# Input codes of a quantised feed-forward layer: two VectorE passes and a DMA transpose in place of a ScalarE pass, TensorE transposes and a PSUM copy

## What is computed

```python
def bit_linear(x, w, b):
    gamma_x = jnp.clip(jnp.max(jnp.abs(x), axis=-1, keepdims=True), 1e-05, None)
    scale_x = 127.0 / gamma_x
    x_dq = jnp.clip(jnp.round(x * scale_x), -128.0, 127.0) / scale_x
    gamma_w = jnp.clip(jnp.mean(jnp.abs(w)), 1e-05, None)
    w_dq = jnp.clip(jnp.round(w / gamma_w), -1.0, 1.0) * gamma_w
    return jnp.einsum('bsd,hd->bsh', x_dq, w_dq) + b
gate = jax.nn.silu(bit_linear(x, gate_w, gate_b))
val = bit_linear(x, val_w, val_b)
return bit_linear(gate * val, out_w, out_b)
...
x = x + jnp.tanh(g_xattn[0]) * cross_attention(layernorm(x), ctx, mask)
x = x + jnp.tanh(g_ffn[0]) * feed_forward(layernorm(x))
```

## Time and profile before

| | |
|---|---|
| median of the runs | 779.17 us (777.58 to 779.35) |
| the profiled execution | 779.99 us, of which the span is 778.2 us |
| TensorE (PE) busy | 712.3 us, 92% of the span |
| VectorE (DVE) busy | 623.1 us, 80% |
| ScalarE (ACT) busy | 534.4 us, 69% |
| GpSimd (POOL) busy | 316.6 us, 41% |
| mean granted clock of TensorE | 0.969 of full speed; full in all of the rows from 1 on |

### The profile page before, as it was taken

The page is one execution under the profiler, slowest core; times in us unless marked ns, Lnnn a source line. Parts: engine busy times, 40 slices in busy tenths (PEclk is TensorE's granted clock), DMA queues, the critical chain, the costliest instruction groups (busy, mean ns, idle before and its releaser), DMA issues.

```text
span 778.2 us, 13495 instructions
## 1 busy us (share of the span) xinstructions
PE 712.3 (92%) x4204; PEld 343.1 (44%) x4253; DVE 623.1 (80%) x1290; ACT 534.4 (69%) x701; POOL 316.6 (41%) x482
## 2 busy tenths in 40 slices
PE   4989756978989999999999999999999999999997
PEld 4434334333534454445444444444444444454443
DVE  6868797687878987798779877987798778778885
ACT  4576878877657865787668856795588657856554
POOL 4310315223553456344653454444544453354340
PEclk9989885989999999999999999999999999999999
DMA  9864426121553344534453354326433542243312
GB/s 323 257 222 123 107 102 205 35 42 41 114 113 79 82 110 94 115 81 103 99 115 81 66 123 101 81 68 126 104 75 83 118 92 65 55 91 80 88 42 67
DMA packets 177385, 81.05 MB, mean 104 GB/s; under 512 B 156595, under 2 KB 156851, under 8 KB 176710
## 3 DMA queue, kind: packets, MB, share of 16 engines
q1 hardware_dynamic: 177350, 80.62, 42.4%
HBM read 38.75 MB, written 10.51 MB: 63 GB/s over the span
## 4 chain that ended last, share of the span: by engine, by line
PE 43%; DVE 26%; issue 11%; ACT 7%; DMA 6%; POOL 3%; another core or an unknown queue 2%; SPq 1%; DVEq 0%; POOLq 0%; ACTq 0%
PE psum L1741 15%; PE psum L1707 12%; PE psum L1732 6%; DVE psum L1227 2%; DMA arena<-x_both 2%; ACT arena L921 2%; PE psum L1936 2%; PE psum L1711 2%; DVE stats L1266 2%; PE psum L1772 2%; DVE xmax L1312 2%; DVE delta L1285 1%; DVE stats L1300 1%; DVE delta L1294 1%
## 5 line engine op out<-in xcount | busy, mean ns | idle before, releaser
L1707 PE MATMUL psum<-ternary,xqT 128*128 128x512 f16 x1024 | 261.4, 382 | 3.3 <-DVE xqT L1257 1.1
L1707 PEld LDWEIGHTS psum<-ternary,xqT 128*128 128x128 f16 x1024 | 98.6, 99 | 119.8 <-issue 5.3
L665 POOL TENSOR_TENSOR rstd<-var_e,minus_half 128x1 f32<-128x1 f32 x64 | 39.8, 621 | 216.9 <-DVE var_e L1278 113.7
L1732 PE MATMUL psum<-ternary,arena 128*128 128x512 f16 x496 | 121.6, 379 | 2.1 <-DMA arena<-arena 2.1
L855 ACT ACTIVATE arena<-psum,dequant 128x512 f32<-128x512 f32 x128 | 86.3, 679 | 48.0 <-PE psum L1711 46.5
L1741 PE MATMUL psum<-wo_hi,arena 128*128 128x512 f16 x256 | 82.6, 384 | 1.0 <-issue 1.0
L1741 PE MATMUL psum<-arena,wq_hi 128*128 128x512 f16 x256 | 77.4, 385 | 3.1 <-DMA arena<-x_both 2.5
L1240 DVE TENSOR_REDUCE hmax<-arena 128x1 f32<-128x1024 f32 x64 | 77.6, 1213 | 0.8
L863 ACT ACTIVATE arena<-arena,round_c,hscale 128x1024 f32<-128x1024 f32 x62 | 73.5, 1235 | 1.9 <-DVE hscale L1252 1.9
L895 ACT ACTIVATE arena<-arena,round_c 128x1024 f16<-128x1024 f32 x62 | 70.8, 1143 | 0.3
L1732 PEld LDWEIGHTS psum<-ternary,arena 128*128 128x128 f16 x496 | 46.4, 98 | 55.0 <-issue 4.4
(11 more groups left out here) (214 smaller groups left out, 1308.5 us busy)
## 6 DMA issues: line engine op xcount, KB each, us to landing
arena<-in_x SPq DMA_DIRECT2D x64, 256.0 KB, 2.8
out<-arena SPq DMA_DIRECT2D x31, 256.0 KB, 2.3
arena<-in_L_ffn_gate_w SPq DMA_DIRECT2D x4, 1024.0 KB, 13.8
arena<-in_L_ffn_out_w SPq DMA_DIRECT2D x3, 1024.0 KB, 4.8
ternary<-in_L_ffn_val_w SPq DMA_DIRECT2D x2, 1024.0 KB, 11.4
kcur<-k_scratch SPq DMA_DIRECT2D x56, 32.0 KB, 2.2
arena<-arena SPq DMA_TRANSPOSE x90, 3.1
ternary<-in_ctx SPq DMA_DIRECT2D x1, 1024.0 KB, 5.4
```

Source lines behind the costliest of these rows:

```text
L1707: ins = M.matmul(ps[:], xqT[:, t % 2, k, :], w[:, k, cols], start=(k == 0), stop=(k == KC - 1 and not biased))
L1732: ins = M.matmul(psO[:], hidT[t % 2][:, k, :], wo2[:, k, :], start=(k == 0), stop=(k == FC - 1))
```

## The change

The codes are made by VectorE in two passes in the new `input_codes`, right behind `input_scale`: the first does what `round_input` did, the second takes the constant off and writes f16 to the new tile `xq16`. SyncE then transposes `xq16` into `xqT` by a DMA (`x_T`). TensorE's four transposes, VectorE's `xq_T` and ScalarE's `round_input` are gone. The product of the inverse scales stays where it was. `gate_val` waits for the codes alone at its start and for the inverse scales ahead of the first bias product.

```diff
+        xq16 = sb("xq16", [P, D], F16)
...
+            def x_T(row, t):
+                last, u = ahead(row, t, -2)
+                wait_alone(sp, s_met_sp, v_done, last, NCH * (u + 1))
+                wait_alone(sp, s_met_sp, xc16_ready, row, t + 1)
+                sp.dma_start_transpose(xqT[:, t % 2, :, :], xq16[:, :]).then_inc(xqT_loaded.sem, 16)
...
+                    x_T(0, 0)
                     sp.wait_ge(s_wtr, 6)
...
+                    update = att if t == NT - 1 else ffn
+                    if update and not (att and t == 2) and not (pre and t == 3):
+                        x_T(*ahead(b, t, 1))
                     if att and t == 2:
                         for u in range(NT):
+                            if u == C_T_AHEAD and update:
+                                x_T(*ahead(b, t, 1))
                             c_T(a, u)
                     if pre and t == 3:
                         h_T(c, 2)
+                        x_T(*ahead(b, t, 1))
...
             def update_inverse(row, t):
-                wait_alone(pool, s_met_pool, xq_tr, last, u + 1)
+                wait_alone(pool, s_met_pool, iv_tr, last, u + 1)
...
-                def round_input(row, t):
-                    wait(act, xq_tr, last, u + 1)
-                    wait(act, xs_ready, row, t + 1)
-                    A.activation(xq32, x1c, ACT.Identity, scale=xscale[:, t:t + 1],
-                                 bias=round_c[:, 0:1]).then_inc(xq_ready.sem, 1)
...
                 def inverse_rows(row, t):
-                    wait(act, xqT_ready, row, t + 1)
+                    wait(act, iv_tr, row, t + 1)
...
-                def xq_T(row, t):
-                    wait(dve, xq_tr, row, t + 1)
-                    V.tensor_scalar(xqT[:, t % 2, :, :].rearrange("p k n -> p (k n)"), half(psT)[:, 0:D], -HALF, None,
-                                    ALU.add).then_inc(xqT_ready.sem, 1)
...
+                def input_codes(row, t):
+                    last, u = ahead(row, t, -1)
+                    wait(dve, xc16_ready, last, u + 1)
+                    wait(dve, xs_ready, row, t + 1)
+                    V.tensor_scalar(xq32, x1c, xscale[:, t:t + 1], ROUND, ALU.mult, ALU.add).then_inc(xq_ready.sem, 1)
+                    wait(dve, xqT_loaded, last, 16 * (u + 1))
+                    wait(dve, xq_ready, row, t + 1)
+                    V.tensor_scalar(xq16[:, :], xq32, -ROUND, None, ALU.add).then_inc(xc16_ready.sem, 1)
...
                     if i == 0:
-                        wait(pe, xqT_ready, b, t + 1)
-                        wait(pe, iT_ready, b, t + 1)
+                        wait(pe, xqT_loaded, b, 16 * (t + 1))
...
-                        if m > 2:
-                            wait(pe, used, b, m - 2)
+                        wait(pe, used, *(b, m - 2) if m > 2 else (b - 1, NT * NCH + m - 2))
...
                         if biased:
+                            if i == 0:
+                                wait(pe, iT_ready, b, t + 1)
...
-                def xq_transpose(row, t):
-                    wait(pe, xq_ready, row, t + 1)
-                    codes = low(xq32)
-                    for k in range(KC):
-                        M.transpose(half(psT)[:, k * P:(k + 1) * P], codes[:, k * P:(k + 1) * P], eye16[:])
+                def inverse_transpose(row, t):
+                    last, u = ahead(row, t, -1)
+                    wait(pe, iT_ready, last, u + 1)
                     wait(pe, iv_part, row, PARTS * (t + 1))
                     M.matmul(psT[:, 2 * P:3 * P], inv_cols[:, t % 2, :], eye_b16[:],
-                             start=True, stop=True).then_inc(xq_tr.sem, 1)
+                             start=True, stop=True).then_inc(iv_tr.sem, 1)
...
+C_T_AHEAD = 2
```

More of the change, by code:

```diff
@@ L347, in build @@
         res_ready = per_row("resid_ready", NT)
-        xq_tr = per_row("xq_transposed", NT)
-        xqT_ready = per_row("xqT_ready", NT)
+        xc16_ready = per_row("x_codes_ready", NT)
+        iv_tr = per_row("inverse_transposed", NT)
+        xqT_loaded = per_row("xqT_loaded", 16 * NT)
         g_done = per_row("gate_product", NT * NCH)
@@ L864, in quant @@
                                      scale=hscale[:, t:t + 1], bias=round_c[:, 0:1]).then_inc(hq_ready.sem, 1)
-                def round_input(row, t):
-                    last, u = ahead(row, t, -1)
-                    wait(act, xq_tr, last, u + 1)
-                    wait(act, xs_ready, row, t + 1)
-                    A.activation(xq32, x1c, ACT.Identity, scale=xscale[:, t:t + 1],
-                                 bias=round_c[:, 0:1]).then_inc(xq_ready.sem, 1)
                 def inverse_rows(row, t):
-                    wait(act, xqT_ready, row, t + 1)
+                    wait(act, iv_tr, row, t + 1)
                     A.copy(inv_rows[:, t % 2, :], psT[:, 2 * P:3 * P]).then_inc(iT_ready.sem, 1)
@@ L962, in first_row @@
                     sum_abs(1, 3)
-                    round_input(0, 0)
                     round_w(0, 2)
@@ L993, in body @@
                     for n in range(NCH):
-                        if n == NCH - 1 and t == 0 and update:
-                            round_input(*ahead(b, t, 1))
                         if ffn:
@@ L1001, in body @@
                             h_high(c, 2)
-                        if n == NCH - 1 and t > 1 and update:
-                            round_input(*ahead(b, t, 1))
                         if att and t == 0:
@@ L1018, in body @@
                         exps(range(2))
-                        if update:
-                            round_input(*ahead(b, t, 1))
                         exps(range(2, NPAIR - 2))
                         exps(range(NPAIR - 2, NPAIR))
-                    if update and t == 1 and not att:
-                        round_input(*ahead(b, t, 1))
                     if pre and t != 2:
@@ L1384, in first_row @@
                     input_scale(0, 0)
+                    input_codes(0, 0)
                     weight_sum(1)
@@ L1394, in first_row @@
                     weight_clip(0, 2)
-                    xq_T(0, 0)
                     weight_round(0, 3)
@@ L1452, in body @@
                                 input_scale(*nxt)
+                                input_codes(*nxt)
                             if ffn and not (out_w_now and t == 1):
@@ L1456, in body @@
                             input_scale(*nxt)
+                            input_codes(*nxt)
                         if n == 3:
-                            if update and not att:
-                                xq_T(*nxt)
                             if ffn:
                                 hidden_max(t, 1)
-                            if update and att and t >= 2:
-                                xq_T(*nxt)
                         if att and t == 0 and n:
@@ L1470, in body @@
                             bound(i)
-                    if update and att and t < 2:
-                        xq_T(*nxt)
                     if out_w_now and t == 0:
@@ L1840, in first_row @@
                     weight_total(1)
-                    xq_transpose(0, 0)
+                    inverse_transpose(0, 0)
                     for g in range(SETUP_BANKS, W_GROUPS):
@@ L1894, in body @@
                     if update:
-                        xq_transpose(*nxt)
+                        inverse_transpose(*nxt)
                     if out_w_now and t == 0:
```

## The result

The changed kernel takes 792.67 us in the median of 4 runs (792.41 to 795.79), the kernel before 779.26 in the same comparison. The ratio is 1.018, with a 95% interval of 1.0146 to 1.0211. The direction was forecast (slower), the size was not: +13 us instead of +3.4, outside the range. The profiled execution took 792.77 us and its span is 791.0, 12.8 longer than before.

What follows compares the result with a forecast made beforehand. A row was taken as mostly TensorE-bound, with tiles 2 and 3 bound by VectorE, then GpSimd. Rows +1.4, setup +1.05, last row +0.94: +3.4 on 779.99, 783.4; less 0.8 for the profiled execution, 782.6 us; range 775.5 to 788.0.

Steps and rivals of the forecast that it cites:

- The step that failed: Tiles 0 and 1: VectorE's net +0.93 us a tile mostly covered, tile 1 by 2.04 us idle; gain 0.70 us a row.
- Rival D: Tiles 0 and 1: VectorE late, tile 0's extra not absorbed, gain falls to 0.2 us; 786.1 us, chance 0.10.
- Rival E: GpSimd's six: each pass blocks GpSimd for its full 0.48 us, 0.96 a tile; 790.2 us, chance 0.05.
- The gain: Tiles 0 and 1: project starts earlier without transposes and round_input; 0.70 us a row taken, bounds 0.2 and 0.92.
- GpSimd's six: Tiles 2 and 3: the passes delay GpSimd's six small instructions by 0.45 us each tile, counted once a row; bounds 0 and 0.96.
- The second pass in f16: VectorE's pass writing f16, in every tile: taken as 0.48 us; both passes 1.05 us, or 1.35 with GpSimd's hold-up.
- The DMA: One 128x512 transpose a tile on SyncE: lands after 2.6 us, bounds 2.4 and 3.1; no cost, or up to 0.4 a row.
- Rival C: Tile 2: the transpose lands after 3.1 us, TensorE waits 0.4 us a row ahead of gate_val(3, 0); 785.4 us, chance 0.12.
- Setup and last row: Outside the seven rows: the passes add 1.05 us to the setup's path and 0.94 us in the last row.

Runs made afterwards that it cites:

- the kernel with both passes moved: Changed kernel with GpSimd's tile 1 wait for the four bounds, passes placed before chunk 3's hidden product in tile 0 and behind hidden_max in tile 3: 781.55 us.
- the kernel with GpSimd's wait: Changed kernel, but in tile 1 GpSimd starts its h subtraction only after VectorE's four bounds; nothing removed: 784.04 us, 1.0059 to the kernel before.
- tiny passes: Changed kernel with both VectorE passes on 8 of 512 columns, other codes constant: 780.59 us; with GpSimd's wait for the bounds as well, 774.89 us.

## Why the prediction was wrong

- **The step that failed** is the one that covered VectorE's extra time in tile 1 by the 2.04 us of the earlier trace rows and booked -0.70 us for tiles 0 and 1. It took the extra of one tile, net, 0.93 us; 2.11 us arrive at the bounds. Tiles 0 and 1 measured 0.00 in place of -0.70, and the weighted stage behind them, booked at nothing, +1.48. How late VectorE is, counted from the row's start: 1.12 us behind the passes of tile 0 (the first `hmax`, at 10.33 before and 11.45 now); 1.95 behind the next instruction, which now lies beside GpSimd's L716 and takes 1.51 us instead of 0.68; 1.24 behind VectorE's next idle time (16.63 and 17.87); 0.98 at the first L1231 of tile 1 (26.77 and 27.75); and 2.11 behind the passes of tile 1. (`xq_T` of tile 1 stood between the bounds and saves nothing ahead of them.)
- **Why VectorE's idle time in tile 0 was no cover.** It is 1.12 us before and still 0.76 now, with VectorE 1.24 us late behind it, because it is a wait for ScalarE, and ScalarE waits for VectorE. VectorE and ScalarE before, then both now:

```profile
491.81 0.75 DVE L1235 SCALAR_TENSOR_TENSOR arena<-psum,dequant,arena 128x512 f32<-128x512 f32 x1 [1.12 <-ACT arena L855]
```

```profile
488.24 0.78 ACT L910 ACTIVATE arena<-psum,bq_c,down_q 128x512 f32<-128x512 f32 x1 [1.23 <-DVE arena L1208]
```

```profile
494.44 1.51 DVE L1206 TENSOR_TENSOR arena<-arena 64x512 f16<-64x512 f32 x1
...
499.61 0.75 DVE L1234 SCALAR_TENSOR_TENSOR arena<-psum,dequant,arena 128x512 f32<-128x512 f32 x1 [0.76 <-ACT arena L871]
```

```profile
496.75 0.78 ACT L918 ACTIVATE arena<-psum,bq_c,down_q 128x512 f32<-128x512 f32 x1 [3.19 <-DVE arena L1207]
```

ScalarE's L918 starts 1.95 us later in the row, the silu that VectorE waits for stands three instructions behind it, and only the missing `round_input` gives some of it back. In the kernel with both passes moved, those of tile 0 stand behind this work, in the idle time itself, and VectorE's `xscale` of tile 1 comes 32.18 us after the row's start instead of 33.50.
- **What the step did not see at all** is that a shift moves an instruction beside another engine's. The cover of 2.04 us was long enough even for the real lateness: in the kernel with GpSimd's wait the bounds end 41.63 us after the row's start, 1.59 later than before, and VectorE still sits idle for 0.59 us ahead of the statistics. But in the changed kernel the bounds slid from just ahead of GpSimd's subtraction to right beside it, and grew from 2.50 to 4.54 us. Rival D named the place (tile 0's extra isn't absorbed, the statistics late), not this mechanism, and priced it at half a microsecond a row. Rival E came near in time (790.2) with a mechanism that the trace refutes: the six are not delayed by whole passes.
- **The gain was sized right where there is no collision.** The row that has no h left to prepare starts at 647.71 (before 636.83). There the bounds take 2.49 us, and the product of tile 1 comes 38.27 us after the start, instead of 39.01: -0.74, forecast -0.70. With the passes of tile 0 moved the steady rows show the same: 18.34 + 19.08 against 18.57 + 19.59. In the changed kernel's steady rows it is 0.00: VectorE's lateness in tile 0 takes it back (TensorE waits 0.45 us for L1231), which is rival D's first half.
- **GpSimd's six: right in kind and in size.** From the first one's start to TensorE's L1716 it is 539.63 to 541.93 = 2.30 us in tile 2 and 557.18 to 559.30 = 2.12 in tile 3; before, 1.75 in both the earlier trace rows. So +0.55 and +0.37 where 0.45 each was taken. In tile 2 single instructions of 0.59 and 0.47 us start beside the passes (539.69, 0.49 us; 540.29, 0.43). Blocks are shorter than a pass, as L665's row had said.

```profile
539.63 0.59 POOL L700 TENSOR_SCALAR inv<-inv_deq,xr 128x2 f32<-128x2 f32 x1 [2.85 <-DVE xr L1310]
540.30 0.47 POOL L704 TENSOR_TENSOR inv_cols<-ones_p,inv 128x6 bf16<-128x6 f32 x1
```

- **The second pass in f16** takes 0.43 us, not 0.48; both with their gaps put 1.12 us between their neighbours, within the 1.05 to 1.35 that were taken.
- **The DMA was right.** The transpose issues in 1.19 us and lands after 2.4, forecast 2.6, and TensorE waits for `xqT` nowhere in the steady row. SyncE costs nothing, by the kernel with the transposes alone. Rival C was wrong for this order, but the kernels with a later start show how near it is: 0.7 to 1.1 us of waiting each.
- **Setup and last row.** The setup's +1.05 cannot be confirmed: the stretch is 0.25 us shorter, in a part that varies by more. From the start of row 6 to the end it is +1.92 us, where +0.2 (row 6) and +0.94 (row 7) were booked; -0.74 in tiles 0 and 1 stands against +2.7 behind. With tiny passes that part is 141.0 us, below the kernel before. So there too it is the passes' time on VectorE, on the chain more often than the two waits of the earlier trace rows let me count; where exactly, no run separates.

Of the miss of 2.1 us a row, 1.62 is the collision and 0.70 the gain of tiles 0 and 1 that VectorE's lateness took; against them stand 0.2, because the other stages without the collision lost 0.68 us (81.50 - 80.82, with nothing in tiles 0 and 1) and 0.90 was booked.

## What to carry to other kernels

Before you count idle time as cover, add up all that arrives there over the whole stretch, and ask what the engine waits for: where its input comes from an engine that waits for it in turn, the idle time moves along and covers little. Before relying on such a cover, lay the other engine's timeline beside the instructions that will slide, most of all VectorE and GpSimd instructions between SBUF tiles: where they will come to lie side by side, one wait may be worth more than the work saved. When a wait vanishes and the time stays, look for a second chain from the same source; here the DMA of the codes and that of h came right behind the inverse scales.

## What the hardware showed that I had not expected

- Four `tensor_scalar` of 128x1024 fp32 take 2.50 us alone and 4.54 beside two GpSimd `tensor_tensor` of 128x512, which themselves go from 1.16 and 1.27 to 1.71 each. With GpSimd held back explicitly the kernel gained 1.2%.
- Two dependent VectorE instructions of 8 columns put 0.61 us between their neighbours, more than half of the 1.12 us at 512 columns.
- A DMA transpose of 128x512 f16 issues in 1.19 us, about the time of the double size, and lands in 2.4 us against 3.1.
